# Attention on one core: TensorE's products in an order that repeats over four steps instead of two

## What is computed

```
def _attention(x, wq, wk, wv, wo, num_heads=16):
    B, S, H = x.shape
    D = H // num_heads
    q = (x @ wq.T).reshape(B, S, num_heads, D)
    k = (x @ wk.T).reshape(B, S, num_heads, D)
    v = (x @ wv.T).reshape(B, S, num_heads, D)
    scale = 1.0 / jnp.sqrt(jnp.float32(D)).astype(x.dtype)
    scores = jnp.einsum('bqhd,bkhd->bhqk', q, k) * scale
    probs = jax.nn.softmax(scores, axis=-1)
    out = jnp.einsum('bhqk,bkhd->bqhd', probs, v).reshape(B, S, H)
    return out @ wo.T
```

## Time and profile before

| | us |
|---|---|
| median of 3 runs | 3388.3 |
| lowest, highest | 3386.01, 3394.44 |
| profiled execution | 3382.51 |
| its span, first to last instruction | 3381.1 |
| attention's heads, from first score to last | about 1270 to 2682 of the span |

### The profile page before, as it was taken

One profiled execution on the slowest core, in us unless ns is written; L12 is line 12 of the kernel. 1 busy time (PEld: TensorE's weight loads), 2 busy tenths in 40 slices (PEclk: granted clock), 3 DMA queues, 4 the chain that ended last, 5 costly groups with the idle time before them and its releaser, 6 DMA issues. The chain is left out here.

```text
span 3381.1 us, 45342 instructions
## 1 busy us (share of the span) xinstructions
PE 2905.4 (86%) x12880; PEld 1119.3 (33%) x12881; DVE 2411.4 (71%) x2674; ACT 1905.4 (56%) x3514; POOL 1090.3 (32%) x652
## 2 busy tenths in 40 slices
PE   5798899889775949999999999999999872999990
PEld 1234334334332512222222222222222262666650
DVE  0699999999996758888888888888888273111113
ACT  3556655665542517777777777777777611222320
POOL 2889778878862530000000000000000045000006
PEclk8999999999998969999999999999999975999995
DMA  1111111111111531111111111111110045111114
GB/s 42 41 50 48 41 57 55 39 48 49 41 48 39 183 94 32 38 39 39 39 39 39 38 34 36 37 39 39 39 39 10 30 144 201 46 45 45 45 37 146
DMA packets 123093, 185.25 MB, mean 55 GB/s; under 512 B 30224, under 2 KB 77968, under 8 KB 122896
## 3 DMA queue, kind: packets, MB, share of 16 engines
q1 hardware_dynamic: 109072, 142.95, 14.9%
q0 software_dynamic: 13824, 39.86, 3.7%
HBM read 138.01 MB, written 44.43 MB: 54 GB/s over the span
## 5 line engine op out<-in xcount | busy, mean ns | idle before, releaser
L1514 DVE TENSOR_REDUCE nmh<-ring 128x2 f32<-128x1024 f32 x1024 | 1188.0, 1218 | 226.5 <-PE ring L1406 225.1
L1387 ACT ACTIVATE prob<-s_ps 128x512 f32<-128x512 f32 x2048 | 1058.6, 605 | 315.9 <-PE s_ps L1427 313.7
L767 DVE TENSOR_TENSOR_SCAN h<-dA,state,bx 128x512 f32<-128x512 f32 x512 | 618.6, 1268 | 116.1 <-ACT dA L606 115.5
L391 POOL TENSOR_TENSOR bx<-u,bb 128x2048 f32<-128x2048 f32 x128 | 578.9, 4527 | 194.1 <-DVE h L767 193.9
L1427 PE MATMUL s_ps<-qs,ks 98*128 98x512 bf16 x2048 | 598.9, 388 | 16.9 <-issue 13.5
L1439 PE MATMUL acc<-prob,vst 128*32 128x512 f32 x4096 | 550.2, 609 | 0.7 <-ACT prob L1387 0.7
L606 ACT ACTIVATE dA<-dt,aneg 128x512 f32<-128x512 f32 x512 | 348.9, 691 | 270.4 <-DVE h L767 270.3
L673 PE MATMUL y_ps<-h,ident 128*128 128x512 f32 x1024 | 482.6, 616 | 1.1 <-DVE h L774 1.1
L1406 PE MATMUL ring<-k,q 64*128 64x512 bf16 x2048 | 368.4, 396 | 43.4 <-DMA k<-parts 23.6
L1427 PEld LDWEIGHTS s_ps<-qs,ks 98*128 98x128 bf16 x2048 | 157.6, 97 | 516.5 <-ACT prob L1387 423.1
L774 DVE TENSOR_TENSOR h<-h,c_ps 128x2048 f32<-128x2048 f32 x128 | 290.2, 2267 | 4.5 <-PE c_ps L652 4.2
(11 more groups left out here) (221 smaller groups left out, 2563.8 us busy)
## 6 DMA issues: line engine op xcount, KB each, us to landing
bb<-b_rows SPq DMA_DIRECT2D x128, 256.0 KB, 3.1
q<-parts SPq DMA_DIRECT2D x256, 64.0 KB, 2.1
parts<-part POOLq DMA_DIRECT2D x48, 256.0 KB, 3.1
qs<-parts SPq DMA_DIRECT2D x192, 64.0 KB, 2.8
ks<-parts SPq DMA_DIRECT2D x192, 64.0 KB, 2.8
xt<-slots_in POOLq DMA_DIRECT2D x72, 128.0 KB, 2.3
slots_out<-yt SPq DMA_DIRECT2D x72, 128.0 KB, 1.7
k<-parts SPq DMA_DIRECT2D x256, 32.0 KB, 2.0
```

Source lines behind the costliest of these rows:

```text
L391: nc.gpsimd.tensor_tensor(bx[:, n % BR], u[:, b], bb[:, n % RB, None, :].to_broadcast([P, KI, CH]), ALU.mult).then_inc(s_bx, 1)
L767: nc.vector.tensor_tensor_scan(h[:, n % HR, d, :], dA[:, d % 2, :], bx[:, n % BR, d, :], state[:, b, n, d:d + 1], ALU.mult, ALU.add).then_ ...
L1387: nc.scalar.activation(prob[:, k % PR, j, :], s_ps[:, tile % SR, :], ACT.Exp, scale=SC).then_inc(s_exp, 1)
L1514: nc.vector.tensor_reduce(nmh[:, slot, t, 2 * s:2 * s + 2], ring[:, s, :, :], AX.X, ALU.max, negate=True).then_inc(s_free[s], 1)
```

## The change

In `head` of TensorE the loop takes four steps a turn instead of two. The products, their number, their operands and their waits are the same; only their order is another. It is described as 14 changes of kind in four steps instead of 16. In the first three of four steps both fills of `ring` now stand together (before: in every second step), in the fourth they stand apart. The last score of the third step is followed by the first score of the fourth, ahead of the values.

```
-                for t in range(0, KT, 2):
+                for t in range(0, KT, 4):
                     k = hh * KT + t
                     scores(n, par, k, 0)
                     scores(n, par, k, 1)
...
                     scores(n, par, k, 3)
                     turn(t)
                     values_of_last(k)
-                    use_ring(t + 1, 0)
                     scores(n, par, k + 1, 0)
                     scores(n, par, k + 1, 1)
                     scores(n, par, k + 1, 2)
+                    use_ring(t + 1, 0)
                     use_ring(t + 1, 1)
+                    scores(n, par, k + 1, 3)
                     values_of_last(k + 1)
-                    scores(n, par, k + 1, 3)
+                    scores(n, par, k + 2, 0)
+                    scores(n, par, k + 2, 1)
+                    scores(n, par, k + 2, 2)
+                    use_ring(t + 2, 0)
+                    use_ring(t + 2, 1)
+                    scores(n, par, k + 2, 3)
+                    turn(t + 2)
+                    scores(n, par, k + 3, 0)
+                    values_of_last(k + 2)
+                    use_ring(t + 3, 0)
+                    scores(n, par, k + 3, 1)
+                    scores(n, par, k + 3, 2)
+                    scores(n, par, k + 3, 3)
+                    use_ring(t + 3, 1)
+                    values_of_last(k + 3)
```

## The result

| | before | after |
|---|---|---|
| median of 4 runs, us | 3387.2 | 3365.0 |
| lowest, highest | 3385.3, 3394.4 | 3358.2, 3366.1 |
| profiled execution, us | 3382.5 | 3366.1 |
| first score of head 0 to first score of head 31, us | 1371.4 | 1350.6 |

The runs of before here are one more than those ahead of the prediction, so their median is another by 1 us. The ratio of after to before is 0.9932, with a 95% interval of 0.9919 to 0.9946: 18 to 27 us faster. The two profiled executions differ by 16.4 us: attention's heads are 20.8 us shorter, and the other stages, which the change doesn't touch, are about 4 us longer in this one trace of after.

What follows compares the result with a forecast made beforehand. TensorE's own list plus waits for ScalarE was taken as the bound. Per head 0.10 + 0.29 + 0.08 = 0.47 us, 14 us over heads 0 to 29, plus 1 for the turns: 15 us, 3373 us, range 3362 to 3388.

Steps and rivals of the forecast that it cites:

- The rival that stood below: A lone score between fills and values costs only 0.22 us: 12 us more saved, 3361 us; chance 0.05.
- The number of changes of kind: TensorE's list: sixteen groups in four steps before and after, none saved; 10.45 us without waits against 10.44 before.
- The middle of a head: Undisturbed four steps take 10.50 us instead of 10.55; 0.10 us gained in a head's two such groups.
- the two places named: Fourth step's first score waits 0.05 us for ScalarE; third pair's second fill, without margin for VectorE, just isn't late.
- t = 12: Wait for ScalarE ahead of the maxima's transposes goes: 0.29 us gained a head, or 0.24.
- t = 0 to 3: First four steps of a head, with the result's transposes: 0.05 + 0.2 - 0.1, less 0 to 0.1; taken as 0.08 us.
- Heads that are written out: Not priced apart: heads 0 to 29 all counted at 0.47 us, head 30 at 0.3, head 31 at nothing.
- The loop's turn: Five turns back of the loop of four heads, TensorE idle about 2.7 us each: 1 us gained in all.
- the reason I gave: At the loop's turn the last product sent is now the values, not a score awaiting an exponential: branch 0.2 to 0.4 us earlier.
- The slower rival: Pairs of fills tie TensorE to VectorE, a late fill costing 0.25 us more: 16 us slower, 3404; chance 0.10.
- the missing margin: Second to third pair's slot 1: VectorE needs 2.83 us and TensorE's own list gives 2.83.

Runs made afterwards that it cites:

- e4: The changed order with exponentials of half a tile (256 of 512 columns), so that ScalarE is never late; 3347.6 us.
- e3: The order of before with exponentials of half a tile (256 of 512 columns), so that ScalarE is never late; 3338.3 us.
- e6: The changed kernel with each fill product taking all 128 array rows instead of 64, exponential's scale a sixteenth; 3441 us in one run.
- e11: The changed kernel with the first score of t = 3 behind the values instead of between transposes and values; 3354.6 us in one run.
- e9: The changed kernel itself, run again on a third chip; 3353.4 us against 3376.6 of before, ratio 0.9929.
- e5: The new order in a head's first four steps alone, the order of before in the other twelve; 3362.4 us, ratio 0.9958 to before.
- e2: Fills together in every step, behind two scores in even steps and three in odd ones; 3404.9 us, ratio 1.0063 to before.
- e8: Every step alike (three scores, both fills, last score, previous step's values), maxima's transposes at t = 12 behind the values; 3351.7 us, ratio 0.9925 to before.

## Why the prediction was right, and where it was off

The total came out within the range, but a head's gain did not: it was put at 0.47 us, between 0.35 and 0.54, and is 0.72. The time of 3365.0 lies just below the 3366 to 3378 that had the chance of 0.60. The rival that stood below, a lone score that costs only its 0.22 us, isn't the reason: it takes 0.31.

- **The number of changes of kind** stays at sixteen, and the list keeps its length: right. Four steps without waits were put at 10.45 us, and e4 has 10.46, of which 0.02 is a wait for VectorE (e3, the old order, 10.44).
- **The middle of a head**: right, 10.50 us. The waits fell from one of 0.05 in every two steps to two small ones in four, at the two places named. That the hundredths agree is partly luck: one wait of 0.05 for ScalarE was laid out and none for VectorE, and it was about 0.03 and 0.02.
- **t = 12**: the gain is right, 0.28 for 0.29, but its parts aren't, so this is luck. The transposes by themselves cost 0.11, not 0.2: without a wait they start 0.44 after the two scores (e3), not 0.54. The waits before were 0.34, and 0.12 of waiting is left, of which the forecast had nothing. Counted from the step's first score the second exponential ends at 1.51 in the trace of after, for a forecast of 1.52, and the transposes start at 1.64. This lag of 0.13 from ScalarE's end is there before too (1.78 to 1.91); heads that are written out have 0.05. Why is open.
- **t = 0 to 3**: this is the step that failed. The net gain was put at 0.08 us between 0.05 and 0.15, and it is 0.32. Three terms were mis-sized. First, the score between transposes and values was charged 0.1 for one change of kind more, and a change between two whole-array products costs nothing (e6, e11). Second, of what stood between two scores and the transposes I took 0.54 as the part without waits, and it is 0.44 (e3), so the wait ahead of them was 0.32 and not 0.23, and some 0.29 of waits fell instead of 0.2. Third, I charged up to 0.1 because the first exponential of t = 1 waits for ScalarE's copy of `acc`. It waits, but not until the copy's end:

```profile
1665.52 0.58 ACT L1362 COPY osb<-acc 128x512 f32<-128x512 f32 x1 [0.16 <-PE acc L1439]
1666.01 1.58 ACT L1387 ACTIVATE prob<-s_ps 128x512 f32<-128x512 f32 x3
```

  ScalarE starts it 0.49 us after the copy's start, the pace of a train, and the fourth score isn't late. The missing 0.24 us a head are some 6 us in the loop's 24 heads, about the whole difference between the forecast and the result. The next two items shift the sum by another -1 and +0.5.
- **Heads that are written out** gain 0.42 us, not 0.72. There ScalarE begins the first exponential of a step 0.49 us after its score instead of 0.43. The trace of before has the same 0.49 in the steps where ScalarE is idle ahead of its first exponential, but there it made nothing late; in the new order the first score of the fourth step waits for it, 0.06 us in each group of four steps. The rest is at t = 12, where the step of before takes 3.36 us outside the loop and 3.43 in it, so there was less to gain. I had counted all heads alike.
- **The loop's turn**: five turns cost 25.0 us before and 23.5 after, 1.5 less, for a forecast of 1. But the same changed kernel has 21.3 in e9, so a difference of this size says little. The idle time alone is more telling. Before, it was 13.5 us in the five turns; after:

```profile
PE s_ps L1427 <- issue: 12.2, 5, 2.6
```

  It is 13.5 again in e5, whose last steps are in the old order. It is 11.9 in e3, where the old order's last score has no exponential to wait for, and 10.5 to 12.7 in the traces of all other kernels that end a head with the values. That fits the reason I gave. It doesn't prove it, since the idle time begins at a modelled end, and of another product in the two orders.
- **The slower rival**: that VectorE can hold up a pair is real (e2), and the third pair comes 0.02 us too soon, as the missing margin threatened. The jump of 0.25 us that made it slower doesn't exist: a late fill costs what it is late, 0.02 us here and 0.23 in e2.

The sum, from the trace: 24 heads in the loop x 0.72 = 17.3, the turns 1.5, the written-out heads 2.0, in all 20.8 us.

## What to carry to other kernels

Where an engine's list is full, an order is to be judged by two sums: the changes of array layout in it, and the waits that it leaves, laid out on one time axis for every engine that gives buffers back. A gain of 0.05 us in a repeating stretch was forecast to the hundredth by such an axis, if with a little luck in its parts; the error came from the one-off places, whose prices had been read from rows that contained waits. Read the price of an operation where nothing is waited for, or make such a place by shortening the engine that is waited for.

## What the runs showed of the hardware

A score to the fills or to the values takes 0.31 to 0.32 us, a score to a score or to a full-row fill (e6) 0.215, and float32 transposes to bfloat16 scores 0.109, the transposes' own pace (e4, e8). Behind the values it is about 0.09: their second four instructions start 0.45 after the first four, and the next product 0.55 after those.
- A train of ScalarE instructions has its starts 0.48 to 0.49 us apart for 512 columns, and a copy from another bank in it counts as one more of the train, though each shows 0.58 to 0.63.
- A fill that VectorE frees too late starts as much later and costs nothing on top, though its load then no longer runs ahead: 0.02 us (after) and 0.23 (e2).
- In heads outside the hardware loop the first exponential of a step began 0.49 us after its score, in the loop 0.43, in both kernels. Why is open.
